# The experts' 40 pairs written out slot by slot instead of in a loop of four

## What is computed

```python
probs = jax.nn.softmax(logits, axis=-1)
rw, sel = jax.lax.top_k(probs, 2)
rw = rw / rw.sum(axis=-1, keepdims=True)
gu = jnp.einsum('nd,edf->nef', x, w_gate_up)     # 256 -> 2 x 128, per expert
g, h = jnp.split(gu, 2, axis=-1)
h = silu(g) * h
expert_out = jnp.einsum('nef,efd,ne->nd', h, w_down, combine)
```

## Time and profile before

| | |
|---|---|
| median of 3 runs | 855.72 us (853.85 to 858.37) |
| the profiled execution | 855.07 us |
| its span, first to last instruction | 853.3 us |
| TensorE busy | 733.0 us, 86% of the span |
| granted TensorE clock, mean share | 0.947 |
| routed experts, first transposes to the last result's start | 620.64 to 746.52 us |

### The profile page before, as it was taken

One profiled execution on the slowest core, in us unless ns is written; L12 is line 12 of the kernel. 1 busy time (PEld: TensorE's weight loads), 2 busy tenths in 40 slices (PEclk: granted clock), 3 DMA queues, 4 the chain that ended last, 5 costly groups with the idle time before them and its releaser, 6 DMA issues. The chain is left out here.

```text
span 853.3 us, 17073 instructions
## 1 busy us (share of the span) xinstructions
PE 733.0 (86%) x5970; PEld 573.1 (67%) x5971; DVE 523.1 (61%) x1158; ACT 400.6 (47%) x777; POOL 360.3 (42%) x664
## 2 busy tenths in 40 slices
PE   2488899898989989899787587999689999999997
PEld 1355576665766656666454466878589999987886
DVE  5276787676876768766670358455534444556667
ACT  3135656455664556645555122443346556632232
POOL 4306346283562835625374023757600000057771
PEclk9789999999999999999987868999889999999999
DMA  5677375673856728466111221977654465357863
GB/s 148 241 272 279 123 256 192 228 247 121 270 176 243 249 105 284 141 246 224 59 62 51 86 75 62 313 250 250 210 184 153 162 191 173 123 188 245 257 213 134
DMA packets 102503, 159.72 MB, mean 187 GB/s; under 512 B 7712, under 2 KB 78368, under 8 KB 98208
## 3 DMA queue, kind: packets, MB, share of 16 engines
q1 hardware_dynamic: 96288, 141.99, 49.4%
q0 software_dynamic: 6144, 16.79, 5.9%
HBM read 86.66 MB, written 71.83 MB: 186 GB/s over the span
## 5 line engine op out<-in xcount | busy, mean ns | idle before, releaser
L622 DVE TENSOR_REDUCE neg_max<-ps_w 128x1 f32<-128x512 f32 (+3 forms) x352 | 200.6, 631 | 68.0 <-PE ps_w L727 67.2
L559 ACT ACTIVATE probs<-ps_w 128x512 f32<-128x512 f32 x320 | 166.2, 616 | 32.7 <-PE ps_w L743 32.1
L410 POOL TENSOR_TENSOR pool_scratch<-minus_half 1x1 f32<-1x1 f32 x190 | 35.1, 185 | 258.9 <-ACT probs L559 221.1
L1110 POOL DMA_INDIRECT ex<-yg_dram,slots x64 | 64.6, 1009 | 155.7 <-DMA yg_dram<-y 136.5
L754 PE MATMUL ps_w<-probs,v_aug 128*32 128x512 f32 (+3 forms) x1024 | 87.8, 490 | 9.5 <-POOL probs L440 9.2
L440 POOL TENSOR_SCALAR_AFFINE_SELECT probs<-probs 128x256 f32<-128x256 f32 (+1 forms) x224 | 94.2, 431 | 0.0
L1098 POOL DMA_INDIRECT xg_dram<-srow,slots x64 | 66.2, 1035 | 52.6 <-DVE slots L1261 27.5
L192 PE MATMUL ps_f<-stacks 128*128 128x512 f32 x176 | 72.7, 413 | 10.3 <-DVE xT_lo_f L1279 7.1
L1127 ACT ACTIVATE silu<-ps_f 128x512 f32<-128x512 f32 (+1 forms) x48 | 28.5, 594 | 103.6 <-PE ps_f L194 103.6
L754 PEld LDWEIGHTS ps_w<-probs,v_aug 128*32 128x32 f32 x1024 | 34.9, 120 | 58.1 <-issue 40.3
L193 PE MATMUL ps_f<-xT_lo_f,stacks 128*128 128x512 f32 x176 | 70.9, 403 | 0.0
(11 more groups left out here) (169 smaller groups left out, 1834.2 us busy)
## 6 DMA issues: line engine op xcount, KB each, us to landing
qk_dram<-projected SPq DMA_DIRECT2D x96, 256.0 KB, 4.1
stacks<-qk_dram SPq DMA_DIRECT2D x16, 1024.0 KB, 7.0
xg_dram<-zeros SPq DMA_DIRECT2D x20, 512.0 KB, 10.5
srow<-xg_dram SPq DMA_DIRECT2D x40, 256.0 KB, 2.8
q_st<-qk_dram SPq DMA_DIRECT2D x8, 1024.0 KB, 4.7
k_st<-qk_dram SPq DMA_DIRECT2D x8, 1024.0 KB, 8.1
projected<-experts SPq DMA_DIRECT2D x16, 384.0 KB, 4.8
yg_dram<-projected SPq DMA_DIRECT2D x20, 256.0 KB, 2.2
```

What stands on the lines that cost most here:

```text
L410: ticks = Ticks(pool, pool_ticks, lambda: pool.tensor_tensor(out=pool_scratch[:, 0:1], in0=minus_half[0:1, 0:1], in1=minus_half[0:1, 0:1], ...
L559: act.activation(probs[:, g, p * PAIR + half * BANK:p * PAIR + (half + 1) * BANK], ps_w[:, plan.bank(kind, which, half), :], ACT.Exp).then ...
L622: dve.tensor_reduce(out=neg_max[u][:, qt, first:first + len(heads)], in_=bank[:, 0:len(heads) * width].rearrange("p (h n) -> p h n", h=len ...
L1110: pool.indirect_dma_start(out=back[:, m, c, :], out_offset=None, in_=yg_rows, in_offset=bass.IndirectOffsetOnAxis(ap=slots[:, c, m:m + 1], ...
```

## The change

The loop and its order of four are gone. Every engine now runs `slot(n)` for n from -1 to 40, in Python, so that all thresholds and buffer numbers are constants; only the experts' numbers stay in registers. A slot n holds, on each engine, at most one step of each kind: the hidden rows of pair n-1, the input of pair n+2, the gates of pair n+1 and the result of pair n-1. The last two slots with input do transposes of the shared expert's next batch instead, which stood in the last four before.

```diff
-    def fours_loop(engine, four_pairs):
-        four_pairs(0, True)
-        with engine.Fori(FOUR, TILE_PAIRS - 2 * FOUR + 1, FOUR) as q:
-            four_pairs(q, True)
-        four_pairs(TILE_PAIRS - FOUR, False)
+    def slots_of_loop(slot):
+        for n in range(-1, TILE_PAIRS + 1):
+            slot(n)
+
+    def is_pair(q):
+        return 0 <= q < TILE_PAIRS
...
 SP:
+        def load_pair(q):
+            if q >= FOUR:
                 sp.wait_ge(m_xT, q - (FOUR - 1))
+            sp.dma_start(xg[:, q % FOUR], xg_pairs[q]).then_inc(moe_in[q % FOUR], 16)
+        def store_pair(q):
             sp.wait_ge(m_y, q + 1)
+            sp.dma_start(yg_pairs[q], y_e[q % FOUR]).then_inc(moe_out[q % FOUR], 16)
-        def four_pairs(q, more):
-            for n in range(FOUR):
-                if more:
-                    load_pair(q + FOUR + n, n)
-                if n >= 1:
-                    store_pair(q + n - 1, n - 1)
-            store_pair(q + FOUR - 1, FOUR - 1)
+        def slot(n):
+            if n + 2 >= FOUR and is_pair(n + 2):
+                load_pair(n + 2)
+            if is_pair(n - 1):
+                store_pair(n - 1)
         def tiles():
...
+            for q in range(FOUR):
+                load_pair(q)
...
 ACT:
+        def slot(n):
+            if is_pair(n - 1):
+                split_h(n - 1)
+            if n >= 0:
+                split_x(n + 2) if is_pair(n + 2) else split_xT(FIRST, [n + 2 - TILE_PAIRS]) if n + 2 < TILE_PAIRS + DK else None
+            if is_pair(n + 1):
+                silu_pair(n + 1)
+            if is_pair(n - 1):
+                result(n - 1)
...
 DVE:
+        def slot(n):
+            if is_pair(n - 1):
+                lower_h(n - 1)
+            if n >= 0:
+                lower_x(n + 2) if is_pair(n + 2) else split_xT(FIRST, [n + 2 - TILE_PAIRS]) if n + 2 < TILE_PAIRS + DK else None
+            if is_pair(n + 1):
+                product(n + 1)
...
 PE:
         def experts_of(q):
-            four = pe.value_load(experts_of_four[0:1, bass.ds(q, 1)], min_val=0, max_val=E ** 4 - 1)
+            four = pe.value_load(experts_of_four[0:1, q:q + 1], min_val=0, max_val=E ** 4 - 1)
...
+        def gate_and_up(q):
+            if q % 2 == 0:
+                experts_of(q)
             pe.wait_ge(m_xT_split, q + 1)
...
+        def slot(n):
+            if is_pair(n - 1):
+                transpose_h(n - 1)
+            if n >= 0:
+                transpose_x(n + 2) if is_pair(n + 2) else transpose_xn(FIRST, [n + 2 - TILE_PAIRS]) if n + 2 < TILE_PAIRS + DK else None
+            if is_pair(n + 1):
+                gate_and_up(n + 1)
+            if is_pair(n - 1):
+                project_down(n - 1)
```

More of the change, by code:

```diff
@@ L1035, in tiles @@
                 sp.wait_ge(scattered[par], SCATTERS * PARITY)
-            for n in range(FOUR):
-                load_pair(n, n)
+            for q in range(FOUR):
+                load_pair(q)
             sp.wait_ge(xT_ready, DK * FIRST)
             load_xn(FIRST)
-            fours_loop(sp, four_pairs)
+            slots_of_loop(slot)
             for n in range(FOUR):
@@ L1145, in first_half, with split_x, silu_pair @@
             shared(b, more, split_expert)
-        def split_x(q, n):
+        def split_x(q):
             act.wait_ge(m_xT, q + 1)
-            act.activation(xgT_hi[:, n % 2, :], ps[:, X_BANK + n % 2, :], ACT.Copy).then_inc(m_xT_hi, 1)
-        def silu_pair(q, n):
+            act.activation(xgT_hi[:, q % 2, :], ps[:, X_BANK + q % 2, :], ACT.Copy).then_inc(m_xT_hi, 1)
+        def silu_pair(q):
             act.wait_ge(m_up, q + 1)
-            if not is_number(q, 0, 1):
+            if q >= 2:
@@ L1161, in result @@
-        def result(q, n):
+            act.activation(hT_hi[:, q % 2, :], ps[:, H_BANK + q % 2, 0:2 * P], ACT.Copy).then_inc(m_hT_hi, 1)
+        def result(q):
             act.wait_ge(m_down, q + 1)
[L1163 to L1183, removed]
+            if q >= FOUR:
+                act.wait_ge(moe_out[q % FOUR], 16 * (q // FOUR))
+            act.activation(y_e[q % FOUR], ps[:, Y_BANK + q % 2, :].rearrange("p (t d) -> p t d", t=2), ACT.Copy).then_inc(m_y, 1)
@@ L1189, in tiles @@
-            fours_loop(act, four_pairs)
+            for q in range(2):
+                split_x(q)
+            slots_of_loop(slot)
         act.wait_ge(args_ready, 2)
@@ L1349, in first_half, with lower_x, product @@
             shared(b, more, split_expert)
-        def lower_x(q, n):
+        def lower_x(q):
             dve.wait_ge(m_xT_hi, q + 1)
-            dve.tensor_tensor(out=xgT_lo[:, n % 2, :], in0=ps[:, X_BANK + n % 2, :], in1=xgT_hi[:, n % 2, :].bitcast(f32), op=ALU.subtract)\
+            dve.tensor_tensor(out=xgT_lo[:, q % 2, :], in0=ps[:, X_BANK + q % 2, :], in1=xgT_hi[:, q % 2, :].bitcast(f32), op=ALU.subtract)\
                .then_inc(m_xT_split, 1)
-        def product(q, n):
+        def product(q):
@@ L1357, in product @@
             dve.wait_ge(m_silu, q + 1)
[L1358 removed]
+            if q >= 2:
                 dve.wait_ge(m_hT, q - 1)
[L1360 to L1363 removed]
+            dve.tensor_tensor(out=h_e[:, q % 2], in0=ps[:, UP_BANK + q % 2, :].rearrange("p (t f) -> p t f", t=2)[:, :, F:2 * F],
+                              in1=silu_e[:, q % 2], op=ALU.mult).then_inc(m_h, 1)
@@ L1364, in lower_h @@
+        def lower_h(q):
             dve.wait_ge(m_hT_hi, q + 1)
-            dve.tensor_tensor(out=hT_lo[:, n % 2, :], in0=ps[:, H_BANK + n % 2, 0:2 * P], in1=hT_hi[:, n % 2, :].bitcast(f32),
+            dve.tensor_tensor(out=hT_lo[:, q % 2, :], in0=ps[:, H_BANK + q % 2, 0:2 * P], in1=hT_hi[:, q % 2, :].bitcast(f32),
                               op=ALU.subtract).then_inc(m_hT_split, 1)
[L1368 to L1383, removed]
+        def slot(n):
[5 more added lines that the diff above has]
+                product(n + 1)
@@ L1385, in tiles @@
         def tiles():
-            for par in range(2):
-                lower_x(par, par)
-            fours_loop(dve, four_pairs)
+            for q in range(2):
+                lower_x(q)
+            slots_of_loop(slot)
         def second_half(b, more):
@@ L1471, in shared, with transpose_x @@
                         last.then_inc(down_ready, 1)
+        chosen = {}
         def experts_of(q):
-            four = pe.value_load(experts_of_four[0:1, bass.ds(q, 1)], min_val=0, max_val=E ** 4 - 1)
[L1476 to L1483, removed]
+            four = pe.value_load(experts_of_four[0:1, q:q + 1], min_val=0, max_val=E ** 4 - 1)
+            chosen[q] = four % E, (four // E) % E
+            chosen[q + 1] = (four // E ** 2) % E, four // E ** 3
+        def transpose_x(q):
+            pe.wait_ge(moe_in[q % FOUR], 16 * (q // FOUR + 1))
+            if q >= 2:
                 pe.wait_ge(m_xT_split, q - 1)
@@ L1494, in gate_and_up @@
                 t, k = divmod(i, DK)
-                last = exact_product(pe, ps[:, UP_BANK + n % 2, t * 2 * F:(t + 1) * 2 * F],
-                                     tuple(v[:, n % 2, i * P:(i + 1) * P] for v in (xgT_hi, xgT_lo)),
-                                     tuple(expert(chosen[t], part, k * 2 * F, (k + 1) * 2 * F) for part in range(2)),
+                last = exact_product(pe, ps[:, UP_BANK + q % 2, t * 2 * F:(t + 1) * 2 * F],
+                                     tuple(v[:, q % 2, i * P:(i + 1) * P] for v in (xgT_hi, xgT_lo)),
+                                     tuple(expert(chosen[q][t], part, k * 2 * F, (k + 1) * 2 * F) for part in range(2)),
@@ L1508, in project_down @@
             pe.wait_ge(m_hT_split, q + 1)
-            if not is_number(q, 0, 1):
+            if q >= 2:
                 pe.wait_ge(m_y, q - 1)
             for t in range(2):
-                last = exact_product(pe, ps[:, Y_BANK + n % 2, t * D:(t + 1) * D],
-                                     tuple(v[:, n % 2, t * P:(t + 1) * P] for v in (hT_hi, hT_lo)),
-                                     tuple(expert(chosen[t], part, DK * 2 * F, EW) for part in range(2)), start=True, stop=True)
+                last = exact_product(pe, ps[:, Y_BANK + q % 2, t * D:(t + 1) * D],
+                                     tuple(v[:, q % 2, t * P:(t + 1) * P] for v in (hT_hi, hT_lo)),
+                                     tuple(expert(chosen[q][t], part, DK * 2 * F, EW) for part in range(2)), start=True, stop=True)
@@ L1537, in tiles @@
         def tiles():
             pe.wait_ge(xT_split, FIRST * DK)
-            for par in range(2):
-                transpose_x(par, par)
+            for q in range(2):
+                transpose_x(q)
             pe.wait_ge(h_done, FIRST * FT)
@@ L1544, in tiles @@
             pe.wait_ge(routed, 1)
-            fours_loop(pe, four_pairs)
+            slots_of_loop(slot)
             pe.wait_ge(m_h, TILE_PAIRS)
```

40 lines of the change are left out of this document (6 added, 34 removed).

## The result

The changed kernel takes **1058.4 us** (1055.26 to 1059.43), against 857.05 us for the kernel before on the same chip: a ratio of 1.237, 95% interval 1.233 to 1.241. The prediction was 1073, range 1020 to 1105. The profiled execution took 1055.26 us, with a span of 1053.5, so 1.8 us lie around it.

A forecast was written before the change was run, and what follows sets the result against it. TensorE was taken as the bound, busy 86% of the span. With 35 periods of 9.08 us, T(39) moves from 738.47 to 953.0; with 3.6 at the end, the shift of 218 us on 855.07 gives 1073 us, range 1020 to 1105.

The forecast's parts named there:

- The ring: Routed pairs 4 to 39: products, result, store, load, next transposes form a loop; 4.03 us besides PE's burst.
- the slower landing: Loads close behind stores in the routed part land in 3.7 us: period 9.98, time 1105 us; within the likeliest case.
- The clock: PE's clock in the routed part: idle nearly 4 us every period, so half clock; period 9.08 us, against 6.76 at full.
- Half clock for nearly the whole part: PE's bursts in the routed part run at 1.2 GHz, 5.05 us each instead of 2.73.
- The mixture: Rival: routed part at mean clock 0.71, work about 3.8 us, period 7.9, time 1028 us; chance 0.12.
- the likeliest one: Half clock nearly throughout the routed part: 1073 us, own range 1055 to 1105; chance 0.76.
- The tail: After T(39): 8.05 us to the last result as before, plus 2.3 and some 1.3 us for half-clock bursts.
- the same work in both kernels: PE's work after T(39) is unchanged, 8.05 us to the last result before, with no load left to wait for.
- Full clock in the ring: Rival: regular bursts keep PE's clock full in the routed part; period 6.76, time 988 us; chance 0.07.
- Loads in time: Rival: SP issues loads early enough for PE's transposes, the 9 us are gained: 846 us; chance 0.02.
- What the change takes away: Routed loop on PE: written-out order could give back about 1.15 us a turn, 9 us over eight turns.

The follow-up runs named there:

- the run with PE kept busy and the early read: Changed kernel plus 24 unused products per PE slot before the waiting transposes, experts' numbers read at the slot's start: 993.3 us.
- one slot earlier: Changed kernel with SP's slot n issuing load n+3 instead of load n+2: 879.4 us.
- the ring cut: Changed kernel with SP's slot n issuing load n+5 instead of load n+2: 845.5 us, and 842.6 us when run once more.

## Why the prediction was right

**The ring.** Each term stood as forecast. Means of the 36 rounds beside the prediction: last product to result 0.04 (0.04), result 0.60 (0.60), its end to the store 0.02 (0.03), store to load 0.42 (0.42), load to transposes 2.88 (2.8 + 0.14); in all 3.96 us against 4.03. The 36 waits sum to 131.5 us by PE's products and 142.3 by its weight loads, forecast 135; T(4) starts at 635.12, forecast 635.2. The last term, the landing of a load close behind a store, had bounds of 2.6 to 3.7; on the mean it is 2.88 with the transposes' start in it, and none of the 36 loads landed later than 3.0, so the slower landing that was put at the end of the range did not show:

```profile
DMA to landing us min/median/max: 2.6/2.8/3.0
```

One reading on the way to the ring was wrong: T(11) does not come after D(8) in the old order but before it, behind D(7). The 5.6 us of room for load 11 were read from the rows and stand, and no term of the sum hangs on that sentence.

**The clock** was the term that was mis-sized. "Half clock for nearly the whole part", 5.05 us a burst, held in 18 of 35 bursts (5.06 in the one shown). One, the first, ran at the full clock, and in 16 the clock came back in the later part, after 10 to 16 products. By the starts of PE's products, with 9.08 forecast and 8.57 measured as the mean period, the 17.8 us by which T(39) came too early (935.21 against 953.0) are made up so, to within 0.3:

- from the first to the last product's start 3.50 us on the mean, instead of 3.78: 35 x 0.28 = 9.8 us
- from the transposes to the first product 0.77 on the mean, instead of 0.86: 3.1 us
- the last product 0.28 instead of 0.41 in these 17 bursts: 17 x 0.13 = 2.2 us
- the way through ACT, SP and DMA: 35 x 0.07 = 2.4 us

The mixture was on the table, and its mean clock, 0.71 by the earlier trace rows, is what came (0.70). Yet it was priced too low: it divided 2.73 us of work by 0.71 and had 3.8, and the bursts took 8.57 - 3.96 = 4.6, which is 2.73 / 0.59. The step that failed is to take the granted clock of a stretch with gaps for that of the work in it: the stretches of the two rounds shown above have 0.50 in the bursts' beginnings and up to 0.95 in the gaps. So the truth lay between the two cases, at the lower end of the likeliest one's own range (a period of 8.6, clock back within some bursts).

By the Trainium skill, TensorE: Matmul & The Clock Gate, section HAM oscillation — how this bites in real kernels, every burst of a kernel that waits for a DMA between short bursts starts at the half clock. The trace agrees for most: four transposes took 1.11 or 1.12 us in 31 of the 36 rounds, against 0.60 at the full clock. In the other five they were shorter, 0.66 to 0.94, and in four of these five the clock fell within the burst, as in this one, whose products stand 0.21 to 0.22 apart from the second to the sixteenth:

```profile
841.00 0.67 PE L1469 MATMUL ps_f<-ident,srow 128*128 128x128 f32 x4 [3.57 <-DMA srow<-xg_dram]
```

**The tail.** From T(39) to the last result it was 948.79 - 935.21 = 13.6 us against 8.05 before, so 5.5 more where 3.6 was estimated. Its burst at the half clock took 2.3 us more, as forecast, but the next ran at the full clock, so the 1.3 us put on that were not spent. In their place came what the forecast had as "the same work in both kernels": by the order in slots only the next batch's transposes, or nothing, stand between the last hidden rows' transposes and the products that read them, and PE waits for VectorE:

```profile
944.72 0.38 PE L192 MATMUL ps_f<-ex,h_hi 128*128 x1 [0.85 <-DVE h_lo L1356]
947.20 0.47 PE L192 MATMUL ps_f<-ex,h_hi 128*128 x1 [1.29 <-DVE h_lo L1356]
```

These two waits are 2.1 us, and the last products behind them ran at the half clock, some 0.6 us more. With T(39)'s shift of 935.21 - 738.47 = 196.7 this gives 202.3; the profiled execution is 200.2 longer than that of before, so 2 us were gained outside the routed part, which no row was sought for. That these 2 us and the tail's excess of 1.9 cancel is luck.

**The rivals.** Full clock in the ring, 988: it did not come by itself, but the run with PE kept busy and the early read measured that case at 993. Loads in time, 846: the condition stated for it, loads two slots earlier at least, was met with three, and gave 845.5; one slot earlier still waited, as stated, though in another rhythm. What the change takes away, 9 us, was near: with the ring cut, 843 to 846 us against 854 to 855 before, 10 to 11 us. The forecast had it as one sum; the loop's turn is 0.46 us of it per turn, the order by slots 0.64.

**What stays open.** Why the clock came back in every second burst, and why this rhythm slipped at some places (two wholly slow bursts in a row from 727.57 and from 822.81 us), no run tells. Nor was two slots of lead run; the one and the three bound it.

## What to carry to other kernels

When a queue's order is written anew, draw for each load the chain of what stands ahead of it on its issuing engine: a load behind a store waits for the store's data, and the slot in which its consumer stands says how much of that is covered. Give the load a lead of at least the whole way from that data to the load's arrival (here 4 us against slots of 2.8), or let another engine issue the stores. And cost a new wait on PE twice, once for itself and once for the slower clock after it: here 148 and some 60 us.

## What the runs showed of the hardware

The clock was not simply low after waits. In bursts of 18 products after 3.3 to 4.1 us of idleness it mostly began at half and in about every second burst was back at full after 10 to 16 products, so that the periods alternate (mostly 8.1 to 8.5 and 8.8 to 9.2 us). Four bursts began at full and were at half from their first or second product on. The granted clock was 0.78 and 0.95 in gaps in which PE did nothing, and 0.50 when the next burst began: in these rounds it followed the work with a delay, and a mean over gaps and bursts (0.70) says too much for the bursts (0.59). Work without use, 3.12 us of it in each wait, held the clock at 0.99 and took 57 us off the time.

PE read its experts' numbers only when a waiting group of transposes ahead of the read had its data: with PE kept busy, the first product came 0.82 to 0.93 us after those transposes with the read behind them, and 0.41 with the read ahead. At the half clock this hardly shows: mostly 0.82 to 0.83 us with the read and 0.76 to 0.77 without, in the changed kernel, so the same read that costs 7.6 us at the full clock costs there about 18 x 0.06 = 1 us by estimate.

SP's step from a store to the load behind it was 0.40 to 0.42 us in 35 of the 36 rounds and 0.76 in one.
